# One linear operation for both heads of a diagonal half, behind both raises

## The reference

```python
x = x + 0.5 * ffn(layernorm(x))          # ffn(x) = x @ W.T + b + (x @ V_r) @ C.T
x = x + attn(layernorm(x))
x = x + 0.5 * ffn(layernorm(x))

def attn(x):                              # 16 heads of 16, B = 4, T = 2048
    q, k, v = split(x @ W_attn)           # each (B, 16, T, 16)
    att = einsum('bhid,bhjd->bhij', q, k) / sqrt(16)
    att = where(causal, att, -inf)
    att = polymax(att)   # s > 0: s*s + 1;  -100 <= s <= 0: 1 - s/100;  else 0;  all / 1000
    y = einsum('bhij,bhjd->bhid', att, v)
    return y @ W_proj
```

## Time and profile before

| | |
|---|---|
| median of 3 runs | 1956.75 us (1953.23 to 1956.96) |
| the profiled execution | 1957.39 us, of which span 1955.6 us |
| busy | PE 85%, ACT 70%, DVE 68%, POOL 68% |
| the chain that ended last | PE 52%, ACT 17%, DVE 15%, issue 8%, POOL 4%, DMA 3% |
| linear parts | 768 on DVE, 256 on ACT |

### The profile page before, as it was taken

One profiled execution on the slowest core, in us unless ns is written; L12 is line 12 of the kernel. 1 busy time (PEld: TensorE's weight loads), 2 busy tenths in 40 slices (PEclk: granted clock), 3 DMA queues, 4 the chain that ended last, 5 costly groups with the idle time before them and its releaser, 6 DMA issues.

```text
span 1955.6 us, 66923 instructions
## 1 busy us (share of the span) xinstructions
PE 1667.1 (85%) x27158; PEld 807.2 (41%) x27158; DVE 1328.0 (68%) x3313; ACT 1363.4 (70%) x2178; POOL 1323.8 (68%) x1419
## 2 busy tenths in 40 slices
PE   4687889898989899898989989898988889898884
PEld 2344334343434444353444435343444444434332
DVE  1465677776767777677777767777677777777652
ACT  1244568787878777777778778776877888886650
POOL 3354558787878767778776768877677767676552
PEclk9898889999999999999999999999999999999996
DMA  2343433332315242343424333341513231413111
GB/s 74 122 135 120 128 102 93 93 104 79 112 50 152 67 118 76 113 117 90 121 59 129 92 101 102 95 133 32 159 50 118 70 95 49 117 39 106 37 36 58
DMA packets 155190, 183.14 MB, mean 94 GB/s; under 512 B 22012, under 2 KB 129660, under 8 KB 152836
## 3 DMA queue, kind: packets, MB, share of 16 engines
q1 hardware_dynamic: 154884, 178.82, 31.3%
HBM read 102.43 MB, written 76.30 MB: 91 GB/s over the span
## 4 chain that ended last, share of the span: by engine, by line
PE 52%; ACT 17%; DVE 15%; issue 8%; POOL 4%; DMA 3%; SPq 0%; ACTq 0%; DVEq 0%; POOLq 0%
PE y_ps L977 19%; PE score L977 16%; PE bank L977 13%; DVE rp L912 9%; ACT rp L820 7%; ACT rp L836 4%; PE bank L1003 3%; ACT rp L840 3%; POOL z L686 2%; DVE lin L918 1%; DMA part_scratch<-parts 1%; ACT lin L826 1%; DVE qk_max L924 1%; DMA out_dram<-x 1%; DVE bnst_ln L937 1%
## 5 line engine op out<-in xcount | busy, mean ns | idle before, releaser
L912 DVE TENSOR_SCALAR rp<-score 128x512 f32<-128x512 f32 (+2 forms) x1728 | 944.2, 574 | 223.4 <-PE score L977 219.7
L977 PE MATMUL score<-qs,ks 96*32 96x512 bf16 (+3 forms) x10240 | 742.8, 354 | 169.5 <-DVE rp L912 86.1
L724 POOL TENSOR_TENSOR rp<-rp 128x1024 f32<-128x1024 f32 (+1 forms) x416 | 755.7, 1828 | 148.5 <-DVE rp L912 137.2
L820 ACT ACTIVATE rp<-score 128x512 f32<-128x512 f32 (+1 forms) x832 | 458.5, 592 | 292.3 <-PE score L977 289.8
L977 PE MATMUL y_ps<-rp,vt 128*16 128x512 f32 (+3 forms) x5120 | 598.6, 539 | 22.1 <-ACT rp L840 14.2
L977 PEld LDWEIGHTS score<-qs,ks 96*32 96x32 bf16 x10240 | 291.6, 96 | 599.0 <-DVE rp L912 314.1
L836 ACT ACTIVATE rp<-rp,rise 128x1024 f32<-128x1024 f32 (+1 forms) x416 | 464.1, 1145 | 1.4 <-POOL rp L699 1.4
L699 POOL TENSOR_SCALAR_AFFINE_SELECT rp<-rp 128x256 f32<-128x256 f32 (+1 forms) x384 | 184.1, 481 | 312.6 <-ACT rp L820 158.4
L840 ACT ACTIVATE rp<-rp 128x1024 f32<-128x1024 f32 (+2 forms) x224 | 291.1, 1305 | 121.3 <-POOL rp L699 67.6
L918 DVE SCALAR_TENSOR_TENSOR lin<-score,slope_mask 128x128 f32<-128x128 f32 x768 | 215.1, 280 | 0.0
L977 PEld LDWEIGHTS y_ps<-rp,vt 128*16 128x16 f32 x5120 | 133.6, 97 | 102.4 <-ACT rp L840 25.5
(11 more groups left out here) (78 smaller groups left out, 1392.9 us busy)
## 6 DMA issues: line engine op xcount, KB each, us to landing
part_scratch<-parts SPq DMA_DIRECT2D x16, 1536.0 KB, 7.5
qs<-part_scratch SPq DMA_DIRECT2D x384, 64.0 KB
ks<-part_scratch SPq DMA_DIRECT2D x384, 64.0 KB, 2.4
state_scratch<-st_new SPq DMA_DIRECT2D x16, 528.0 KB
st<-state_scratch SPq DMA_DIRECT2D x64, 132.0 KB
x_sb<-in_L_attn_x_dram SPq DMA_DIRECT2D x16, 512.0 KB, 4.3
x_scratch<-x SPq DMA_DIRECT2D x16, 512.0 KB, 5.3
qT_scratch<-qkT SPq DMA_DIRECT2D x16, 512.0 KB, 3.9
```

Source lines behind the costliest of these rows:

```text
L724: pool.tensor_tensor(half, half, half, ALU.mult).then_inc(squared["pool"], 1)
L820: nc.scalar.activation(rp[T % RP_BUFS][:, 2 + v, off:CH], score[H % S_BUFS][:, v, off:CH], ACT.Relu).then_inc(raised["act"], 1)
L912: nc.vector.tensor_scalar(rp[T % RP_BUFS][:, 2 * u + v, off:CH], score[H % S_BUFS][:, v, off:CH], 0.0, RISE, ALU.max, ALU.add).then_inc(ra ...
L977: return nc.tensor.matmul(*args, start=start, stop=stop, skip_group_check=True)
```

## The change

The two raises of a diagonal half stay one operation for each head with a signal each. The linear parts of the two heads become one operation over both heads, issued behind the second raise, with one signal for the half in place of two. PE's wait for the linear part of half `H` before it writes half `H + 2` is the same for both heads: the half's one signal.

```diff
@@ -246,7 +246,7 @@
             raised[who] += 2
             o.raised.append((who, raised[who]))
             if is_diag(T):
-                lin[who] += 2
+                lin[who] += 1
                 o.lin[2 * T + u] = (who, lin[who])
         squared["act"] += 1
         squared["pool"] += shared(T)
@@ -439,9 +439,9 @@
             who, value = o.raised[H]
             eng.wait_ge(raised[who], value - 1 + v)
 
-        def wait_lin(eng, H, v=1):
+        def wait_lin(eng, H):
             who, value = o.lin[H]
-            eng.wait_ge(lin_done[who], value - 1 + v)
+            eng.wait_ge(lin_done[who], value)
 
         def split(eng, b, i, step):
 
@@ -819,12 +819,12 @@
                         act.wait_ge(qk_done, 2 * H + v + 1)
                         nc.scalar.activation(rp[T % RP_BUFS][:, 2 + v, off:CH], score[H % S_BUFS][:, v, off:CH],
                                              ACT.Relu).then_inc(raised["act"], 1)
-                        if is_diag(T):
-                            D = diag_index(T)
-                            if D >= L_BUFS:
-                                act.wait_ge(pv_done, diag_tile(D - L_BUFS) + 1)
-                            nc.scalar.activation(lin[D % L_BUFS][:, 2 + v, :], score[H % S_BUFS][:, v, off:off + P],
-                                                 ACT.Copy, scale=SLOPE, bias=ONE).then_inc(lin_done["act"], 1)
+                    if is_diag(T):
+                        D = diag_index(T)
+                        if D >= L_BUFS:
+                            act.wait_ge(pv_done, diag_tile(D - L_BUFS) + 1)
+                        nc.scalar.activation(lin[D % L_BUFS][:, 2:4, :], score[H % S_BUFS][:, :, off:off + P],
+                                             ACT.Copy, scale=SLOPE, bias=ONE).then_inc(lin_done["act"], 1)
                 for T in o.squares.get(s, ()):
                     off = TILES[T % NT][2]
                     if is_diag(T):
@@ -911,12 +911,12 @@
                         dve.wait_ge(qk_done, 2 * H + v + 1)
                         nc.vector.tensor_scalar(rp[T % RP_BUFS][:, 2 * u + v, off:CH], score[H % S_BUFS][:, v, off:CH],
                                                 0.0, RISE, ALU.max, ALU.add).then_inc(raised["dve"], 1)
-                        if is_diag(T):
-                            D = diag_index(T)
-                            if u == 0 and D >= L_BUFS:
-                                dve.wait_ge(pv_done, diag_tile(D - L_BUFS) + 1)
-                            nc.vector.scalar_tensor_tensor(lin[D % L_BUFS][:, 2 * u + v, :], score[H % S_BUFS][:, v, off:off + P],
-                                                           ONE / SLOPE, slope_mask[:, 0, :], ALU.add, ALU.mult).then_inc(lin_done["dve"], 1)
+                    if is_diag(T):
+                        D = diag_index(T)
+                        if u == 0 and D >= L_BUFS:
+                            dve.wait_ge(pv_done, diag_tile(D - L_BUFS) + 1)
+                        nc.vector.scalar_tensor_tensor(lin[D % L_BUFS][:, 2 * u:2 * u + 2, :], score[H % S_BUFS][:, :, off:off + P],
+                                                       ONE / SLOPE, slope_mask[:], ALU.add, ALU.mult).then_inc(lin_done["dve"], 1)
                 for x in o.empties.get(s - 1, ()):
                     if x.kind in ("qT", "kT"):
                         j = x.i if x.kind == "qT" else KC + x.i
@@ -1056,7 +1056,7 @@
                     if H >= S_BUFS:
                         wait_raised(pe, H - S_BUFS, v)
                         if is_diag((H - S_BUFS) // 2):
-                            wait_lin(pe, H - S_BUFS, v)
+                            wait_lin(pe, H - S_BUFS)
                     ins = strips(score[H % S_BUFS][:, v, off:CH], ks[:, head, P * kb:P * kb + P],
                                  qs[:, head, CH * c + off:CH * c + CH])
                     ins.then_inc(qk_done, 1)
```

## The result

The changed kernel takes 1980.29 us (median of 6 runs, 1976.41 to 1985.14), the kernel before 1957.21 us beside it (6 runs, 1953.23 to 1958.84): a ratio of 1.012, interval 1.0101 to 1.0139. It is 23 us slower; I had forecast 11. The direction and the wide range (1949 to 1984) held, the forecast's own range (1961 to 1979) was missed by 1.3 us, the size was off by a factor of two, and most of it comes from a place that the forecast did not look at. The profiled execution took 1976.41 us, span 1974.7.

The account below looks back on a forecast made before the run. PE, busy 85% of the span, was taken to set the time. 1957.4 us plus 11.7 for later refills minus 1 for smaller terms gave 1968 us; forecast's own range 1961 to 1979, wide range 1949 to 1984.

Parts of the forecast that it names:

- The wait that moves: At a late diagonal half both heads' refill waits for one linear part, so PE's program is 0.15 us later.
- The sum over an iteration: Six of eight late places pass on 0.15 us, less ACT's gain: 0.78 us an iteration, +11.7 us over fifteen.
- the two that I had counted: Late places at 835.02 and 878.14, taken as covered by PE's waits for ACT at 836.37 and 880.65.
- Rows 4's loop: DVE waits for PE's `state` job (910.75), PE for the raise behind it (911.82); nothing between takes up the 0.15 us.
- fifteen iterations like this one: Scaling of one iteration's 0.78 us loss, read from 829 to 909 us, to the whole run: +11.7 us.
- The smaller terms: Earlier second raises start POOL's mask and ACT's square sooner: 8.3 us at most, counted as 1 us gained; other effects nothing.
- DVE's relief: One linear part in place of two saves DVE 0.06 us for each of 384 halves, 23 us, nearly all into idle time.
- the second rival: Prediction's pointer for the skill's fewer-operations rule (DVE saves 48 us); second in its list stands DVE starves.
- the rival meant, relief: Raises behind diagonal halves end earlier, half of 39 us of engine savings passes on: faster, 1945 us; chance 0.18.
- The rival that DVE starves: 128 DVE halves of shared diagonal tiles wait for the refill; one in four passes on, 19 us more: 1987 us; chance 0.12.

Follow-up runs that it names:

- 5: Changed kernel with one more wait on POOL: before its square it waits until VectorE's operation on `shift` is done; 1957.2 us, ratio 1.0021.
- 6: Kernel before with one more wait on POOL: before its square it waits until VectorE's operation on `shift` is done; 1953.0 us, ratio 1.0001.
- 9: Changed kernel with the operation on `shift` moved from VectorE to POOL and ACT writing the negative mean; 1956.0 us, ratio 1.0013.
- 10: Kernel before with the operation on `shift` moved from VectorE to POOL and ACT writing the negative mean; 1947.8 us, ratio 0.9974.
- the two controls: 6 and 10: the kernel before with the added POOL wait (1953.0 us), and with the operation on `shift` moved to POOL (1947.8 us).
- 3: Against the kernel before, only ACT's halves make one linear operation over both heads, VectorE keeps one for each head; 1957.6 us, ratio 1.0043.
- 8: Kernel before with both linear parts behind both raises, still one operation and one signal for each head; 1980.9 us, ratio 1.0139.
- 4: Against the kernel before, only VectorE's halves make one linear operation over both heads, ACT keeps one for each head; 1968.3 us, ratio 1.0080.
- the eight kernels above: The kernel before (1957.21 us), the changed kernel (1980.29 us) and the kernels of experiments 3 to 8.
- 7: Kernel before with two reciprocals of 128x4 into an unused tile in front of VectorE's operation on `shift`; 1970.3 us, ratio 1.0090.
- 1: Changed kernel without VectorE's operation on `shift`; POOL normalises by subtracting the mean, then multiplying by the reciprocal; 2037.6 us, ratio 1.0433.
- 2: Kernel before without VectorE's operation on `shift`; POOL normalises by subtracting the mean, then multiplying by the reciprocal; 2042.7 us, ratio 1.0460.

## Why the prediction was wrong in size

*The wait that moves: right.* 0.15 us at the late half, both heads behind one signal, DVE's idle time passed on as drawn, PE late 114 + 14 times for a linear part where the rows before had 125.

*The sum over an iteration: mis-sized, too high.* Forecast: 0.78 us. With the holds away, iterations 4 to 10 differ by 0.4 us in the profiles of experiments 5 and 6 and by nothing in those of 9 and 10. Among those in which the clock stayed at 1.00 throughout it is 0.2 us in both pairs (112.8 against 112.5, and 112.5 against 112.3). In iteration 6 of the changed kernel the 0.15 us do appear one by one against the kernel before, at the refills of positions 30, 36, 42, 48 and 56, and as much in all, 0.16 to 0.23 us each time, is given back at positions 39, 44, 53 and 60: the waits in between took them up more often than the two that I had counted. Rows 4's loop, which I took as proof that nothing takes them up, did pass its 0.15 us on to 911.82, and gave it back at position 60, behind the rows that I read. And "fifteen iterations like this one" was wrong for the last: iterations 12 to 14 got shorter. Over the whole execution the change costs 4.2 us (5 against 6) to 8.2 us (9 against 10) by the medians, in place of 11.7. Where these arise is not shown: in the profiles iterations 1 to 14 together differ by only +0.1 and -0.7 us, and the profiled executions of the two controls were 7 and 10 us slower than their medians.

*The smaller terms: this is the step that failed.* I wrote that POOL's mask starts 0.20 us earlier because the second raise no longer stands behind a linear part, and counted that as a gain of 1 us; I had no term for an operation of VectorE that waits for one of POOL. The earlier POOL is the loss: some 15 of the 23 us by experiments 9 and 10 (23 less 8.2), 19 by 5 and 6. Its square now starts 0.09 us before VectorE's `shift` in place of 0.10 us behind its start, and such an operation of VectorE ends only with POOL's. That was to be read in the trace of before: the operation on `shift` has a maximum of 1464 ns at a median of 163, line 865 has 21 of 48 over 0.6 us, and the earlier trace rows shows only operations that read PSUM. The rows have 1.39 us for one that takes 0.16 alone. The Trainium skill has the rule, in "Advanced Engine Details and Errata", section "GPSIMD Details": GpSimd shares one read and one write interface with VectorE and conflicts with VectorE's operations that have two inputs in SBUF, or run in a mode with two ports. The trace agrees for the operation on `shift`, which has two inputs in SBUF. I asked of each engine who waits for its signals, and not which of its operations run only when another engine is not running.

*Why POOL is ahead.* The traces show it, in iteration 6. There POOL masks behind ACT's second raise, and the lead of that mask reaches the square by way of ACT's square and `parts` (line 459). Before:

```profile
833.60 0.41 POOL L699 TENSOR_SCALAR_AFFINE_SELECT rp<-rp 128x256 f32<-128x256 f32 x1 [2.68 <-ACT rp L820]
```

And in the changed kernel:

```profile
839.30 0.41 POOL L699 TENSOR_SCALAR_AFFINE_SELECT rp<-rp 128x256 f32<-128x256 f32 x1 [2.92 <-ACT rp L820]
```

The score matmul in front of the square (position 17, at 852.80 and 858.80) comes 19.20 us behind this mask before, 19.50 with the change, 19.38 in experiments 3 and 8 and 19.32 in 4. The square itself starts 0.95 us behind that matmul before, 0.70 with the change, 0.80 in 3, 0.79 in 8 and 0.86 in 4; the operation on `shift` starts at 0.85, 0.80, 0.80, 0.85 and 0.86. So ACT's own order brings POOL 0.15 to 0.18 us forward, PE's later refill behind VectorE 0.09 to 0.12, and they add up. The first is the 0.20 us that I had forecast.

*DVE's relief: as costed.* One operation over both heads takes 415 ns, 56 us less in durations. VectorE's busy time is 24 to 26 us lower where the holds are away (5 against 6, 9 against 10), for the 23 forecast; with the holds it is 14. None of it is seen in the time. (My text ties the skill's rule to the second rival; the rival meant, relief, stands first.) The rival that DVE starves named 1987 us, 7 from the result, but by a mechanism that experiments 5 and 9 leave 4 to 8 us for. That 1980 us lies in my wide range is luck: its bounds came from a linear part of 0.28 to 0.56 us, which measured 0.415.

The account, from the two profiles, whose spans differ by 19.1 us: the attention starts 5.2 us earlier in the changed kernel's (94.7 in place of 99.9 us, in front of all that was changed). Iterations 1 to 10 lose 27.0: ten are held in place of one, nine more at about 2.7 us each make 24 (the 26 held ones among iterations 4 to 10 of the eight kernels above average 115.4 us, the 30 free ones 112.7), and the refill and scatter are the rest. Iterations 0 and 11 lose 1.7, iterations 12 to 14 give back 1.9, and what follows 2.7. Shown by experiment is that the loss goes with the hold (5, 9), comes without the change (7) and comes with the order alone (8). Not shown is why the clock falls behind some holds and not behind others, and where the last 4 to 8 us arise.

## What to carry to other kernels

Where a small operation of VectorE with two SBUF inputs, or one like line 865 that adds a constant from SBUF to SBUF, stands near a long one of POOL, look at its longest duration against its median, not at the mean: if the longest ends with POOL's operation, the kernel sits on a race, and any edit that moves one of the two by 0.2 us can cost or gain more than what it was made for. Take such an operation off VectorE, or put a wait in POOL's program, before measuring other changes. When a forecast says "this engine is now a little earlier", name what it is now beside.

## What the runs showed of the hardware

- VectorE's 128x4 operation with two inputs in SBUF takes 0.16 us alone and up to 1.48 us (experiment 3) where it starts behind the start of POOL's square of 768 columns, which takes 1.47 us; in the changed kernel's profile each of 12 ended 0.02 us behind POOL's. The addition of a constant to 128x4 in SBUF is held alike (up to 1.68 us, ending 0.02 to 0.03 us behind POOL's square). The reciprocal of 128x4 (96 more of them in experiment 7, 13 within a square) never took over 0.18 us.
- Which of the two starts first decides, to a few nanoseconds: in experiments 3 and 4 the operation was free with the square up to 0.005 us ahead and held with it 0.006 us ahead or more. Straight behind a reciprocal (experiment 7) it was free up to 0.049 and held from 0.055 us on.
- POOL's normalisation of 128x256 takes 0.55 us as multiply, then add, and 1.22 us as subtract, then multiply (experiments 1 and 2).
- Behind a hold, with PE idle for 1.78 us and busy for 2.15 us out of 4, the granted clock was 0.50 for about 3 us in iteration 6 of the changed kernel, and stayed at 1.00 in iteration 4, with 1.79 us and 2.21 out of 4. Over eight profiles it fell behind 19 of 26 holds in iterations 4 to 10.
